# A four-layer attention and feed-forward kernel: four edits to the order of work and to one projection's arithmetic

## The reference, cut to what matters

```python
x = x + _L0_xattn_ref(_layernorm(x), k, fside_S2_0, ctx_2048, ctx_2048, 8)   # long convolution over 512 columns
x = x + _L0_ffn_ref(_layernorm(x), gate_w, w1, b1, w2, b2, ...)             # 8 experts, best 2, and a shared one
x = x + _L1_xattn_ref(_layernorm(x), ctx_2048, itok, W_kvc, W_dq, W_uq, W_qr, W_uk, W_kr, W_uv, W_o)
x = x + _L1_ffn_ref(_layernorm(x), proj1, proj1_bias, proj2, proj2_bias, gate_w)

# _L0_ffn_ref: the choice of experts
top_logits, top_idx = jax.lax.top_k(xf @ gate_w, 2)
top_gates = jax.nn.softmax(top_logits, axis=-1)

# _L1_xattn_ref, 16 heads
kv_c = kv @ W_kvc
q_c = q @ W_dq                                  # the queries' first projection
q_nope, q_rope = q_c @ W_uq, q_c @ W_qr
good = (k_ids <= qs) & (k_ids >= qs - LOOKBACK) # the mask, from seg_id
attn = softmax(where(good, scores * scale, NEG)); out = (attn @ v) @ W_o
```

## Time and profile before

| what | us |
|---|---|
| median of 3 runs | 3108.35 (3108.01 to 3108.9) |
| the profiled execution, as timed | 3110.47 |
| its span, from the first to the last instruction | 3108.7 |
| TensorE busy in it | 3083.8 (99%) |
| VectorE, ScalarE, GpSimd busy | 2167.0, 1347.9, 1181.5 |
| granted TensorE clock | 1.00 of full speed |

### The profile page before, as it was taken

How to read it: one execution, slowest core, us unless ns; L and a number is a source line. 1 busy time by engine, 2 the same in 40 slices (tenths; PEclk the granted TensorE clock), 3 DMA queues, 4 the chain that set the end, 5 groups by cost and what they waited for, 6 DMA issues and landing times.

```text
span 3108.7 us, 50216 instructions
## 1 busy us (share of the span) xinstructions
PE 3083.8 (99%) x18455; PEld 2681.0 (86%) x18455; DVE 2167.0 (70%) x5511; ACT 1347.9 (43%) x3298; POOL 1181.5 (38%) x1197
## 2 busy tenths in 40 slices
PE   9999999999999899999999999999999999999999
PEld 6777777899999789999999999999998888888887
DVE  8899898655555788888888888888887433333332
ACT  4656555333444455555555555555555211111111
POOL 9999999354444422222222322223201011111110
PEclk9999999999999999999999999999999999999999
DMA  4444432398777521111111111111102200000000
GB/s 153 132 146 126 147 111 85 100 326 274 237 229 242 196 68 49 44 46 42 48 49 48 44 46 49 48 49 38 46 22 67 73 28 28 28 28 28 28 14 14
DMA packets 124978, 277.72 MB, mean 89 GB/s; under 512 B 18312, under 2 KB 18960, under 8 KB 124736
## 3 DMA queue, kind: packets, MB, share of 16 engines
q1 hardware_dynamic: 95712, 178.54, 18.2%
q0 software_dynamic: 29024, 95.97, 9.4%
HBM read 170.04 MB, written 104.42 MB: 88 GB/s over the span
## 4 chain that ended last, share of the span: by engine, by line
PE 94%; DVE 3%; POOL 1%; DMA 1%; ACT 1%; issue 0%; SPq 0%; POOLq 0%; DVEq 0%
PE g_PH L2513 4%; PE g_PH L2515 4%; PE g_PH L2514 4%; PE g_O L2529 4%; PE g_O L2527 4%; PE g_O L2528 4%; PE t_U L1785 4%; PE f_Y L544 4%; PE f_Y L545 4%; PE f_Y L547 4%; PE t_U L1786 4%; PE t_U L1787 4%; PE t_T L1761 3%; PE f_Y L539 2%; PE t_PO L1771 2%; PE t_S L1750 2%
## 5 line engine op out<-in xcount | busy, mean ns | idle before, releaser
L1914 ACT ACTIVATE t_pr<-t_sm,t_nb 128x256 f32<-128x256 f32 x512 | 256.6, 502 | 409.6 <-DVE t_nb L2124 409.6
L2298 POOL TENSOR_TENSOR t_r<-t_r 128x256 f32<-128x256 f32 x128 | 94.5, 739 | 729.6 <-DVE t_r L2103 409.6
L2585 DVE CAST g_hh<-g_hf 128x512 fp32r<-128x512 f32 x128 | 55.7, 435 | 433.6 <-PE g_O L2529 432.1
L2556 ACT ACTIVATE g_hf<-g_PH,b1g 128x512 f32<-128x512 f32 x128 | 88.2, 689 | 492.7 <-PE g_PH L2515 492.7
L1344 POOL TENSOR_TENSOR c_kf<-c_vt,c_ct 128x512 f32<-128x512 f32 x256 | 284.0, 1125 | 5.9 <-ACT c_vt L775 3.0
L2134 DVE TENSOR_SCALAR t_pr<-t_pr,t_rw 128x256 f32<-128x256 f32 x512 | 239.0, 467 | 18.1
L544 PE MATMUL f_Y<-c_kh,c_th 128*128 128x512 f32 x540 | 250.8, 465 | 0.0
L547 PE MATMUL f_Y<-c_kl,c_th 128*128 128x512 f32 x540 | 213.7, 396 | 0.7 <-DVE c_kl L1062 0.7
L545 PE MATMUL f_Y<-c_kh,c_tl 128*128 128x512 f32 x540 | 213.4, 395 | 0.0
L1785 PE MATMUL t_U<-t_voh,t_oth 128*128 128x512 f32 x512 | 202.4, 395 | 0.0
L2513 PE MATMUL g_PH<-g_xh,g_w 128*128 128x512 f32 x512 | 202.0, 395 | 0.0
(11 more groups left out here) (352 smaller groups left out, 9901.5 us busy)
## 6 DMA issues: line engine op xcount, KB each, us to landing
xs<-c_zero SPq DMA_DIRECT2D x71, 256.0 KB, 4.7
f_xg<-xs SPq DMA_DIRECT2D x71, 256.0 KB, 3.7
ys<-f_yt POOLq DMA_DIRECT2D x71, 256.0 KB, 3.8
f_xg<-xn SPq DMA_DIRECT2D x40, 256.0 KB, 4.9
c_xt<-x SPq DMA_DIRECT2D x32, 256.0 KB, 3.5
c_cr<-ctx SPq DMA_DIRECT2D x32, 256.0 KB, 3.9
c_ct<-ctxh SPq DMA_DIRECT2D x32, 256.0 KB, 4.9
c_t<-kt SPq DMA_DIRECT2D x32, 256.0 KB, 5.0
```

## The change

Four edits.

1. **Front.** `parts` has no exception any more for `(u, mb) = (0, 2)`: in heads 10, 11, 18, 19, 26 and 27 that block goes in parts too. The choice is split: `choose` keeps the first two instructions in place, `mark` (three instructions) follows three heads later, `gates` five heads later, and ScalarE's exponential stands three block steps later, in head 10, 18 and 26.
2. **Ramp.** SyncE's load `wqrb` and `factors(5)` wait for VectorE's first added rows (`V["mix", 0, 0]`); `weights(4)` comes after the wait for the last expert rows, in banks of its own (`m.T`, `m.PU[1]`), and the filler is 20 instead of 26. ScalarE's and VectorE's parts of `wqrb` come after `weights(5)`, and batch 0's mask is GpSimd's.
3. **Projection in parts.** From batch 2 on `qcomp` is 24 float32r matmuls of 256 columns instead of 8 float32 ones. ScalarE's `turned` writes the rounding to `xTh` (the place of `xT`) and the full rows to `xo`, GpSimd subtracts (`turned`, `xTl` in the place of `xo`), and `qcomp` waits for it. `wdq` is split once, in steps 10 to 12 of batch 0. `residual` now waits for `qcomp` of batch b + 1.
4. **Steps.** From batch 1 on `keys` moves from step 5 to 2, `values` from 6 to 3, the two `turn` from 2 and 3 to 6 and 7, and VectorE's `mask` from step 4 to step 13, the fourteenth.

```diff
@@ parts
     if mb == 2 and u == 0:
-        return h > 2 and not (h > 9 and h % 8 in (2, 3))
+        return h > 2
@@ scalar_front, in the loop over h, u, lb
-                if u == 1 and lb == 3 and h > 8 and h % 8 == 1:
+                if u == 0 and lb == 2 and h > 8 and h % 8 == 2:
                     choose(h // 8 - 1)
@@ vector_front: choose(c) ends behind "gap"; mark(c) is the rest of it
                 if u == 1 and lb == 3 and h > 8 and h % 8 == 1:
                     choose(h // 8 - 1)
-                if u == 0 and lb == 1 and h > 8 and h % 8 == 2:
+                if u == 1 and lb == 3 and h > 8 and h % 8 == 4:
+                    mark(h // 8 - 1)
+                if u == 1 and lb == 3 and h > 8 and h % 8 == 6:
                     gates(h // 8 - 1)
@@ sync_attention
     factors(4)
     w.wait_ge(*K.VE["y2", TILES - 1])
+    w.wait_ge(*V["mix", 0, 0])
+    factors(5)
     sp.dma_start(m.wqr[:, 1, :], d["wqrb"]).then_inc(*Q["tw1"]("rb"))
-    factors(5)
-    w.wait_ge(*V["mix", 0, 0])
     context(1)
@@ tensor_attention
     def qcomp(b):
         w.wait_ge(*A["xT", b, 1])
+        if b >= PARTS:
+            w.wait_ge(*A["wdqh"])
+            w.wait_ge(*V["wdql"])
+            w.wait_ge(*G["xl", b, 1])
         M = take("qcomp", b)
         for z in range(2):
+            o, c = M[:, 256 * z:256 * z + 256], slice(128 * z, 128 * z + 128)
             for k in range(4):
+                if b >= PARTS:
+                    pe.matmul(o, m.wdqh[:, k, c], m.xTh[:, k, :], start=k == 0, stop=False)
+                    pe.matmul(o, m.wdqh[:, k, c], m.xTl[:, k, :], start=False, stop=False)
+                    i = pe.matmul(o, m.wdql[:, k, c], m.xTh[:, k, :], start=False, stop=k == 3)
+                    continue
-    for h in range(5):
+    for h in range(4):
         weights(h)
     krope(0)
-    keep_busy(pe, m.PU[0], ident, 26)
+    w.wait_ge(*K.VE["y2", TILES - 1])
+    weights(4)
+    keep_busy(pe, m.PU[0], ident, 20)
@@ scalar_attention, turned(b, t)
+        if b >= PARTS:
+            w.wait_ge(*Q["to"]["out", b - 2])
+            w.wait_ge(*V["wdql"])
+            w.wait_ge(*A["wdqh"])
+            copy(rows_whole(m)[:, :, 128 * t:128 * t + 128], psum("turn", b, t)[:, :]...).then_inc(*A("xf", b, t))
@@ vector_attention
     krope(0)
-    rope_weights()
-    mask(0)
+    weights(4)
     weights(5)
+    rope_weights()
@@
-            if h == (4 if b else 7):
+            if h == (13 if b else 7):
                 mask(b + 1)
-            if b and h == 5:
+            if b and h == 2:
                 keys(b + 1)
@@ gpsimd_attention
+    def turned(b, t):
+        c = slice(128 * t, 128 * t + 128)
+        w.wait_ge(*A["xf", b, t])
+        gp.tensor_tensor(m.xTl[:, :, c], rows_whole(m)[:, :, c], f32(m.xTh[:, :, c]), ALU.subtract)...
+            if b and h in (7, 8):
+                turned(b + 1, h - 7)
```

More of the change, by code:

```diff
@@ L1255, in vector_front @@
             choose(3)
+            mark(3)
         if n == 6:
@@ L1463, with rows_whole @@
           5: lambda b: [("turn", b, 0)], 6: lambda b: [("turn", b, 1)], 9: lambda b: [("qcomp", b)]},
-         {2: lambda b: [("turn", b, 0)], 3: lambda b: [("turn", b, 1)], 5: lambda b: [("keys", b)], 6: lambda b: [("values", b)],
-          7: lambda b: [("krope", b)], 9: lambda b: [("qcomp", b)]})
+         {2: lambda b: [("keys", b)], 3: lambda b: [("values", b)], 6: lambda b: [("turn", b, 0)],
+          7: lambda b: [("krope", b), ("turn", b, 1)], 9: lambda b: [("qcomp", b)]})
+PARTS = 2
+def rows_whole(m):
+    return m.xo[:, :, :].rearrange("p a (k c) -> p (a k) c", c=256)
 def misc_order():
@@ L1837, in tensor_attention @@
                 krope(b + 1)
+            if h in ((6, 7) if b else (5, 6)):
+                turn(b + 1, h - (6 if b else 5))
             if h == 9:
@@ L1940, in weights @@
         w.wait_ge(*P["f", h])
-        copy(m.voh[:, h, :], psum("wv", h)[:, :]).then_inc(*A("voh", h))
+        copy(m.voh[:, h, :], (m.PU[1] if h == 4 else psum("wv", h))[:, :]).then_inc(*A("voh", h))
     w.wait_ge(*K.PE["m2", TILES - 1])
@@ L1957, in scalar_attention @@
     weights(5)
+    rope_weights_b()
     qcomp(0)
@@ L1969, in scalar_attention @@
         if b + 1 < B:
-            if h in ((2, 3) if b else (5, 6)):
-                turned(b + 1, h - (2 if b else 5))
-            if b and h == 5:
+            if b and h == 2:
                 keys(b + 1)
-            if h == (6 if b else 2):
+            if h == (3 if b else 2):
                 values(b + 1)
+            if h in ((6, 7) if b else (5, 6)):
+                turned(b + 1, h - (6 if b else 5))
+            if b == 0 and h == 10:
+                w.wait_ge(*P["f", NH - 1])
+                w.wait_ge(*P["qcp", 1])
+                copy(m.xTl[:, :, :], m.wdq[:, :, :]).then_inc(*A("wdqt"))
+            if b == 0 and h == 12:
+                w.wait_ge(*V["wdql"])
+                copy(m.wdqh[:, :, :], f32(m.xTl[:, :, :])).then_inc(*A("wdqh"))
             if h == 9:
@@ L2219, in vector_attention @@
                 krope(b + 1)
+            if b == 0 and h == 11:
+                w.wait_ge(*A["wdqt"])
+                ve.tensor_tensor(m.wdql[:, :, :], m.wdq[:, :, :], f32(m.xTl[:, :, :]), ALU.subtract).then_inc(*V("wdql"))
             if h == 9:
@@ L2293, in power, with mask @@
         gp.tensor_tensor(m.rs[:, t, :], m.rs[:, t, :], K.mhalf, ALU.pow).then_inc(*G("rs", b, t))
+    def mask():
+        w.wait_ge(*Q["tsg"]["sg", 0])
+        w.wait_ge(*V["xn", 0, 1])
+        gp.tensor_copy(m.sgf[:, 0:2], m.sgi[:, :]).then_inc(*G("sgf", 0))
+        w.wait_ge(*G["sgf", 0])
+        gp.tensor_scalar(m.sgf[:, 2:4], m.sgf[:, 0:2], 8.0, None, ALU.subtract).then_inc(*G("sgl", 0))
+        w.wait_ge(*V["kr3", 0])
+        w.wait_ge(*G["sgl", 0])
+        w.wait_ge(*G["iota"])
+        for t in range(2):
+            M = m.mk[:, 0, t, :]
+            if t:
+                w.wait_ge(*G["mk", 0, 0])
+            gp.tensor_scalar(m.mt[:, :], m.iota, m.sgf[:, t:t + 1], NEG, ALU.is_gt, ALU.mult).then_inc(*G("mka", 0, t))
+            gp.tensor_scalar(M, m.iota, m.sgf[:, 2 + t:3 + t], NEG, ALU.is_lt, ALU.mult).then_inc(*G("mkb", 0, t))
+            w.wait_ge(*G["mkb", 0, t])
+            gp.tensor_tensor(M, M, m.mt[:, :], ALU.add).then_inc(*G("mk", 0, t))
     def rotate(n):
@@ L2314, in gpsimd_attention @@
     power(0, 1)
+    mask()
     rotate(0)
```

63 lines of the change are left out of this document (43 added, 20 removed).

## The result

The changed kernel takes **3125.66 us** in the median of five runs (3122.89 to 3126.4), the kernel before 3108.35 beside it: a ratio of 1.0051, 95% interval 1.004 to 1.0063. It is 17.3 us slower where 7.1 us faster was forecast.

The account below looks back on a forecast made before the run. TensorE, busy 3083.8 of 3108.7 us, was taken as the bound, with VectorE only 12 us to spare a batch. Terms -2.1 - 1.9 - 3.5 - 8.7 + 9.1 = -7.1 us gave 3101.3 us, range 3092 to 3114.

Parts of the forecast that it names:

- The choice of experts: Front: with the exponential three block steps later, three TensorE waits of 0.7 us for `c_xT` go, -2.1 us.
- what is late next is nothing on TensorE's side: Front, choice of experts: `mark` and `gates` at their new places make TensorE wait for nothing; no cost counted.
- Parts in the front: Front: six blocks, each used twice, go to three float32r matmuls, saving 12 x 0.155 us, -1.9 us.
- these heads become like the others: Front: VectorE can absorb one more subtraction a head; if that cover failed, `kl` late by at most 0.95 us, six times.
- The ramp: Before the attention: with SyncE's late loads delayed, the last store lands sooner; -3.5 us, from 0 to -4.
- The projection: `qcomp` in 14 batches from 2 on: 24 float32r matmuls take 2.83 us instead of 3.45, -8.7 us.
- The mask: Step 13, batches 1 to 13: mask delays `ptl`, TensorE stalls 0.55 to 0.95 us, taken as 0.7; +9.1 us.
- the old collision: Step 13 before: VectorE's scaling took 1.17 us instead of 0.35, ending 0.15 us after GpSimd's two-input operation.
- the second collision: Step 14: VectorE's delayed last scaling waits for GpSimd's next two-input operation, 1.29 us long.
- The second: Rival: mask delay hits a second GpSimd operation, 1.57 us a batch; sum +4.2, 3112.5 us; chance 0.30.
- The third: Rival: GpSimd's one-input operations block VectorE too, 2.3 us a batch; +13.3, 3121.7 us; chance 0.05.
- What would show it: Signs: shorter `qcomp`, no `c_xT` waits, earlier store and turning, some 9 us of `ptl` waits, batch 0.1 us longer.

Follow-up runs that it names:

- late_exp: Kernel before, with ScalarE's exponential three block steps later and the gates at the end of head 12; 3112.42 us, ratio 1.0012.
- parts_only: Kernel before, with only the exception in `parts` dropped and the choice of experts where it was; 3112.91 us, ratio 1.0014.
- projection_whole: Changed kernel with light heads at 13 to 15, 21 to 23, 29 to 31, mask in step 8 and float32 projection; 3104.43 us, ratio 0.9988.
- mask_rows_early: Kernel before, with the mask of batches 2 to 15 in step 13 and GpSimd's first expert rows one step earlier; 3121.41 us, ratio 1.0044.

## Why the prediction was wrong, step by step

**The choice of experts** (-2.1 forecast). The failed step is "what is late next is nothing on TensorE's side", with its reason, that `mark` and `gates` stand where the whole of `choose` stood and made no wait but the one through ScalarE. The waits behind heads 9, 17 and 25 did go, and heads 10, 18 and 26 are 1.14 us shorter each. But I put the marking and the gates at nothing without looking at what GpSimd does beside them. At the old place it held VectorE for 1.47 us, because the exponential kept GpSimd back; without the exponential it takes 3.3 to 3.5 there (`late_exp`) and 2.93 at the new place, and heads 14 to 16 are 3.1 us longer behind it and the gates. Part of VectorE's lateness at the old place was moreover hidden by heads 10 and 11 being light: without that the waits are 1.34 to 1.61 us instead of 0.7 (`parts_only`).

**Parts in the front** (-1.9). The saving of 0.155 us a use is there: periods of -0.15 us at heads 12, 20 and 28. The failed step is "these heads become like the others"; they were the ones that had the choice. I had priced the failure of the cover with 0.95 us six times, and judged the cover by VectorE's mean of 90% in the front. The two edits of the front together took the light heads away and set the choice beside heads that had never been light: +4.4 instead of -4.0 us.

**The ramp** (-3.5). Right mechanism: the store lands sooner when SyncE's queue is quiet. Two sizes were off: the store fell to 5.3 us in the mean and not to 3.8, and the comparison was with one run of 8.18 us where seven give 7.1. The traces alone show -5.1 and would have confirmed the term by luck.

**The projection** (-8.7). Right: 2.84 us for 24 matmuls, 0.62 us a batch in `projection_whole` as well, nothing for the copies.

**The mask** (+9.1). Right place, right wait, right 1.57 us that TensorE leaves, right 2.5 us for the undisturbed mask. Mis-sized was what GpSimd adds. I took the old collision's length (0.8 us over the scaling's 0.35) and up to 0.4 more. Measured over the undisturbed durations: the small scalar operation +0.33, the first long one +1.09, the one behind it +0.15, so 1.57 in the mask, while the two scalings got back 0.70. The net is 0.87 us on 2.1, a delay of 2.94 and a stall of 1.39 us instead of 0.7. To this comes the second collision, 0.28. The term is 13 x 1.67 = +21.7.

**The rivals.** The second had the sign, the mechanism and nearly the price of a batch, 1.57 us against 1.67, though it put more into the second collision (0.62) and less into the first. The third (one-input operations of GpSimd hold VectorE for their whole length) is wrong as a rule: a scaling that began 0.03 us behind one of 1.57 us ended after 0.81 us. The page "SBUF — State Buffer" of the Trainium skill, section "Who interferes with whom", has the full exclusion; for the two-input operation the trace agrees (VectorE ends 0.15 us behind it), for the one-input one it does not. No rival spoke of the front, which is why even the upper end of 3114 us was too low: rival 2 with the front as measured would have been 3112.5 + 8.4 = 3120.9.

**What would show it.** 24 records in 2.8 us, and no wait for `c_xT` behind heads 9, 17 and 25: seen. The landing 4 to 5 us after issue: 5.8. The turning at about 1039: 1046.51, since the front did not end 4 us earlier but 4.4 later. Waits only for `ptl` in step 14, some 20 us under the second rival: 15.9 us by the waits, 18 by the steps' lengths. A batch 0.1 us longer: 1.05.

## What to carry to other kernels

A table of exceptions in a tuned kernel may be the cover of something that stands elsewhere; before dropping it, ask which engine it makes light, and in which stretch, rather than what it costs. A wait that names an engine's instruction names the last link: move that instruction alone and see whether the wait goes or walks one place on, and look at what it was holding back: here the exponential kept GpSimd off VectorE's marking. Price a small instruction by its row beside the other engines' work at its new place, not by its size. Put work into an engine's queue where the time between its result and the user is longer than the work and its collisions together, in pieces if need be, and compare with several runs of the kernel before where a DMA's landing is in the sum.

## What was not expected of the hardware

VectorE's scaling of 128 x 256 takes 0.35 us, up to 0.81 beside a one-input operation of GpSimd, and 1.2 when it starts just behind the start of a two-input one. Even an operation on 128 x 2 values took 0.50 us beside the former, instead of 0.17. VectorE's two-input operations on 128 x 64 values, 0.22 us alone, took 0.95 to 1.30 beside two-input ones of GpSimd.

Equal code is not equally long in stretches with DMA: from head 31 to the last expert matmul the profiles differ by up to 3.4 us, and in the ramp the last store by 2.6 us. The batches of one kernel, with little DMA, repeat to 0.01 us where TensorE does not wait; in `mask_rows_early` they differ by 1.2 us, since the moment when a gather lands decides which of VectorE's operations meets GpSimd's.
